# The last pair's evictions, additions and output sums in halves, two evictions shared by ACT and VectorE

## The reference

```
x = x + conv(x, w0) + ctx0(cond) + bias            # grouped conv, 4 groups, 9 taps
x = x + agg_w1(cond) @ x + agg_b1(cond)            # 128x128 matrix per sequence, a softmax blend of 8 experts
x = x + conv(x, w2) + ctx2(cond) + bias
x = x + agg_w3(cond) @ x + agg_b3(cond)
```

## Time and profile before

| | |
|---|---|
| median of 3 runs | 2497.8 us (2497.75 to 2498.95) |
| the profiled execution's own time | 2493.67 us |
| its span | 2491.9 us |
| TensorE busy | 2460.8 us, 99% |
| VectorE busy | 2136.1 us, 86% |
| ACT busy | 1523.4 us, 61% |
| DMA, mean over the span | 143 GB/s |

### The profile page before, as it was taken

The page is one execution under the profiler, slowest core; times in us unless marked ns, Lnnn a source line. Parts: engine busy times, 40 slices in busy tenths (PEclk is TensorE's granted clock), DMA queues, the critical chain, the costliest instruction groups (busy, mean ns, idle before and its releaser), DMA issues.

```text
span 2491.9 us, 99092 instructions
## 1 busy us (share of the span) xinstructions
PE 2460.8 (99%) x45256; PEld 1402.0 (56%) x45256; DVE 2136.1 (86%) x796; ACT 1523.4 (61%) x1116; POOL 32.0 (1%) x28
## 2 busy tenths in 40 slices
PE   7999999999999999999999999999999999999998
PEld 3444444444555555555666666666666666666664
DVE  6988988889889889889889888898898898898883
ACT  5566666666666666666666666666666666666665
POOL 5000000000000000000000000000000000000000
PEclk9999999999999999999999999999999999999999
DMA  9444444444444444444444454444444444444433
GB/s 361 149 145 150 126 132 159 130 126 157 138 126 145 149 126 137 152 132 126 150 145 126 137 157 128 127 159 135 126 150 144 126 142 150 129 128 154 139 95 120
DMA packets 186682, 357.23 MB, mean 143 GB/s; under 512 B 12754, under 2 KB 143834, under 8 KB 154010
## 3 DMA queue, kind: packets, MB, share of 16 engines
q1 hardware_dynamic: 184824, 352.50, 45.2%
q10 hardware_dynamic: 1826, 4.23, 0.5%
HBM read 205.69 MB, written 150.99 MB: 143 GB/s over the span
## 4 chain that ended last, share of the span: by engine, by line
PE 97%; DMA 1%; ACT 1%; DVE 1%; issue 0%; SPq 0%; ACTq 0%
PE psum L373 61%; PE psum L441 35%; DMA mix_dram<-y 1%; DMA out<-outb 0%; ACT y L576 0%; DVE h L730 0%; PE psum L300 0%; ACT outb L625 0%; DVE y L727 0%; PE psum L347 0%; DVE diff L695 0%; DVE shared L738 0%; DVE y L738 0%; DVE y L750 0%; ACT y L612 0%
## 5 line engine op out<-in xcount | busy, mean ns | idle before, releaser
L373 PE MATMUL psum<-diff,prod_w 32*64 32x512 f32 x28672 | 1684.0, 588 | 8.0 <-ACT y L576 2.5
L373 PEld LDWEIGHTS psum<-diff,prod_w 32*64 32x64 f32 x28672 | 908.1, 131 | 684.4 <-issue 401.9
L695 DVE TENSOR_TENSOR diff<-xin 128x2052 f32<-128x2052 f32 x256 | 994.0, 3929 | 288.4 <-PE psum L373 288.4
L441 PE MATMUL psum<-y,mixw 32*64 32x512 f32 x16384 | 1020.1, 588 | 5.5 <-ACT y L576 3.4
L441 PEld LDWEIGHTS psum<-y,mixw 32*64 32x64 f32 x16384 | 545.8, 131 | 371.2 <-issue 221.1
L695 DVE TENSOR_TENSOR diff<-x 128x2055 f32<-128x2055 f32 x256 | 571.2, 2299 | 4.7 <-ACT x L664 4.7
L625 ACT ACTIVATE outb<-psum,bias_now 128x2048 f32<-128x2048 f32 x129 | 252.2, 1956 | 197.9 <-PE psum L441 196.3
L664 ACT ACTIVATE x<-psum,bias_now 128x2048 f32<-128x2048 f32 x128 | 252.8, 1975 | 195.4 <-PE psum L441 195.4
L603 ACT COPY shared<-psum 128x2048 f32<-128x2048 f32 x128 | 239.1, 1868 | 170.4 <-PE psum L373 169.5
L748 DVE TENSOR_TENSOR y<-y,shared 128x2048 f32<-128x2048 f32 x128 | 293.1, 2290 | 38.2 <-ACT y L614 38.2
L616 ACT COPY y<-psum 128x2048 f32<-128x2048 f32 x128 | 239.2, 1869 | 93.6 <-PE psum L373 93.6
(11 more groups left out here) (61 smaller groups left out, 83.3 us busy)
## 6 DMA issues: line engine op xcount, KB each, us to landing
out<-outb SPq DMA_DIRECT2D x127, 1024.0 KB, 4.8
xin<-x SPq DMA_DIRECT2D x126, 1024.0 KB, 6.8
mixw<-mix_dram SPq DMA_DIRECT2D x508, 128.0 KB, 5.5
mix_dram<-shared SPq DMA_DIRECT2D x8, 1024.0 KB, 12.5
mix_dram<-y SPq DMA_DIRECT2D x8, 1024.0 KB, 12.0
xin<-x ACTq DMA_DIRECT2D x2, 1024.0 KB, 10.9
y<-experts ACTq DMA_DIRECT2D x2, 512.0 KB, 4.6
prod_w<-conv_w SPq DMA_DIRECT2D x4, 256.0 KB, 7.9
```

The source lines that it names most:

```text
L373: return pe.matmul(psum[cols, half, g, :], prod_w[v][at, kind, s, cols], moving, start=start, stop=stop, skip_group_check=True)
L441: mm = pe.matmul(psum[cols, half, r, :], mixw[home][at, b, g, cols], y[home][at, :, g, b, :], start=g == 0, stop=g == GROUPS - 1)
L695: nc.vector.tensor_tensor(into(kind), in0, in1, op).then_inc(diff_ready[v], 1)
```

## The change

All of it is in the steps from the first mixing of the last pair (63) on. TensorE's order of matmuls, the number of matmuls and all that is computed stay as they are.

- **x2 of sequence 1**: ACT evicts phases 0 and 1 (signal `x2_ready`), VectorE phases 2 and 3 by `tensor_scalar` (signal `x2_upper`, in `last_diffs`). TensorE waits for both before conv, ACT for `x2_upper` too before it overwrites `bias_now`.
- **BOTH** is added in two halves of columns (phases 0 and 1, then 2 and 3), with a signal each; conv waits for the second half behind its fourth set (`second`). The counts for SIGNED and ONLY_ODD go up by one.
- **half_mix(1, 1)** waits only for line 612's copy at first, for 614's before the TRAILING rows.
- **take_sums** copies the second result half in two pieces, the first at `conv_done` 7.
- **outputs** makes four half operations (groups 0 and 1, groups 2 and 3) with a signal each; `half_mix(0, 0)` waits for the third at first, for the fourth before the TRAILING rows.
- **The last eviction**: ACT evicts phases 0 and 1, VectorE phases 2 and 3 (`last_out`, signal `out_upper`), both over all m. Each of the two stores waits for both. SP stores the upper half of the positions, ACT issues the store of the lower half.

```diff
@@ -138,6 +138,8 @@
...
         x2_ready = sem("x2_ready")
+        x2_upper = sem("x2_upper")
+        out_upper = sem("out_upper")
         out_ready = sem("out_ready")
@@ -195,6 +197,15 @@
...
             return {BOTH: diff2[:, 0], SIGNED: diff2[:, 1], ONLY_EVEN: diff0[:, 0], ONLY_ODD: diff0[:, 1]}[kind]
+
+        def x2_of(b, phases):
+            into = x2[:].rearrange("p (j c) -> p j c", j=PAR)[:, :, 0:PH * T]
+            into = into.rearrange("p j (r b m) -> p j r b m", r=PH, b=PB)[:, :, phases, b, 0:R]
+            return into, psum[:, b, :, :].rearrange("p r (j m) -> p j r m", j=PAR)[:, :, phases]
+
+        def out_of(b, phases):
+            return (outb[:, b, :].rearrange("p (m j r) -> p m j r", j=PAR, r=PH)[:, :, :, phases],
+                    psum[:, b, :, :].rearrange("p r (j m) -> p m j r", j=PAR)[:, :, :, phases])
@@ -243,10 +254,9 @@
...
                         if whole(i) and i == PAIRS + 1 and b == PB - 1:
-                            for part in range(2):
-                                sp.wait_ge(out_ready, PB * PAIRS + part)
-                                at = slice(part * L // 2, (part + 1) * L // 2)
-                                sp.dma_start(out[B - 1, :, at], outb[:, b, at]).then_inc(out_stored[b], 16)
+                            sp.wait_ge(out_ready, PB * PAIRS)
+                            sp.wait_ge(out_upper, 1)
+                            sp.dma_start(out[B - 1, :, L // 2:L], outb[:, b, L // 2:L]).then_inc(out_stored[b], 16)
                             continue
@@ -367,6 +377,9 @@
...
+            def nothing():
+                pass
+
             def conv_tile(v, kind, half, s, g, cols, start=False, stop=False):
@@ -386,7 +399,7 @@
...
-            def conv(v, n, a_free, b_free, diffs, late, halves=(A, B_HALF)):
+            def conv(v, n, a_free, b_free, diffs, late, halves=(A, B_HALF), second=nothing):
@@ -397,6 +410,7 @@
...
                 wide_set(v, BOTH, A, 0, TRAILING, start=True)
+                second()
                 wide_set(v, BOTH, A, 2, LEADING)
@@ -462,11 +476,14 @@
...
-            def half_mix(b, home, late):
+            def half_mix(b, home, late, second=nothing):
...
                 late()
-                for g in range(1, GROUPS):
+                mix_set(1, b, b, 1, LEADING, home)
+                second()
+                mix_set(1, b, b, 0, TRAILING, home)
+                for g in range(2, GROUPS):
                     mix_set(1, b, b, g, LEADING, home)
@@ -475,9 +492,6 @@
...
                 mix_set(m, B_HALF, 1, GROUPS - 1, TRAILING).then_inc(mix_done[m], 1)
-
-            def nothing():
-                pass
@@ -498,14 +512,15 @@
...
                 half_mix(0, 1, lambda: mix_tail(0))
+                pe.wait_ge(x2_upper, 1)
                 conv(1, n, (x2_ready, PB * PAIRS), (out_ready, PB * (n - 1) + 1),
-                     (PRODUCTS * n + 1, PRODUCTS * n + 2, PRODUCTS * n + 4), lambda: half_mix_tail(0, 1),
-                     halves=(B_HALF, A))
-                pe.wait_ge(sums_taken[1], COPIES * n + 2)
-                half_mix(1, 1, lambda: conv_tail(1, A))
-                pe.wait_ge(y_ready[1], 2 * PAIRS)
+                     (PRODUCTS * n + 1, PRODUCTS * n + 3, PRODUCTS * n + 5), lambda: half_mix_tail(0, 1),
+                     halves=(B_HALF, A), second=lambda: pe.wait_ge(diff_ready[1], PRODUCTS * n + 2))
+                pe.wait_ge(sums_taken[1], COPIES * n + 1)
+                half_mix(1, 1, lambda: conv_tail(1, A), lambda: pe.wait_ge(sums_taken[1], COPIES * n + 2))
+                pe.wait_ge(y_ready[1], 2 * n + 3)
                 pe.wait_ge(mix_loaded[0], MIX_LOADS * (PAIRS + 1))
-                half_mix(0, 0, lambda: half_mix_tail(1, 1))
+                half_mix(0, 0, lambda: half_mix_tail(1, 1), lambda: pe.wait_ge(y_ready[1], 2 * n + 4))
                 pe.wait_ge(out_ready, PB * n)
@@ -612,25 +627,28 @@
...
                 nc.scalar.copy(into[:, 0, 2:4], psum[:, A, 2:4, :]).then_inc(sums_taken[v], 1)
+                if whole(n) and v == 1 and n == PAIRS - 1:
+                    act.wait_ge(conv_done[v], done + 7)
+                    nc.scalar.copy(into[:, 1, 0:2], psum[:, B_HALF, 0:2, :]).then_inc(sums_taken[v], 1)
+                    act.wait_ge(conv_done[v], done + 8)
+                    nc.scalar.copy(into[:, 1, 2:4], psum[:, B_HALF, 2:4, :]).then_inc(sums_taken[v], 1)
+                    return
                 act.wait_ge(conv_done[v], done + 8)
...
-            def give_out(i, b, parts=1):
+            def give_out(i, b, phases=slice(0, PH)):
                 n = i - 2
...
                     act.wait_ge(out_stored[b], 16 * n)
-                for part in range(parts):
-                    at = slice(part * R // parts, (part + 1) * R // parts)
-                    nc.scalar.activation(
-                        outb[:, b, :].rearrange("p (m j r) -> p m j r", j=PAR, r=PH)[:, at],
-                        psum[:, b, :, :].rearrange("p r (j m) -> p m j r", j=PAR)[:, at], ACT.Identity,
-                        bias=bias_now[:, b, 1:2]).then_inc(out_ready, 1)
+                nc.scalar.activation(*out_of(b, phases), ACT.Identity, bias=bias_now[:, b, 1:2]).then_inc(out_ready, 1)
...
                         act.wait_ge(x2_ready, PB * i)
+                        if whole(i) and i == PAIRS:
+                            act.wait_ge(x2_upper, 1)
                     else:
@@ -647,7 +665,10 @@
...
                     else:
-                        give_out(i, 1, parts=2)
+                        give_out(i, 1, phases=slice(0, PH // 2))
+                        act.wait_ge(out_ready, PB * PAIRS)
+                        act.wait_ge(out_upper, 1)
+                        act.dma_start(out[B - 1, :, 0:L // 2], outb[:, 1, 0:L // 2]).then_inc(out_stored[1], 16)
                     return
@@ -659,10 +680,9 @@
...
                         act.wait_ge(mix_done[0], PB * i + b + 1)
-                        into = x2[:].rearrange("p (j c) -> p j c", j=PAR)[:, :, 0:PH * T]
-                        into = into.rearrange("p j (r b m) -> p j r b m", r=PH, b=PB)[:, :, :, b, 0:R]
-                        nc.scalar.activation(into, psum[:, b, :, :].rearrange("p r (j m) -> p j r m", j=PAR),
-                                             ACT.Identity, bias=bias_now[:, 2 * PB + b, 0:1]).then_inc(x2_ready, 1)
+                        phases = slice(0, PH // 2 if whole(i) and i == PAIRS - 1 and b == 1 else PH)
+                        nc.scalar.activation(*x2_of(b, phases), ACT.Identity, bias=bias_now[:, 2 * PB + b, 0:1]
+                                             ).then_inc(x2_ready, 1)
@@ -744,13 +764,52 @@
...
                 dve.wait_ge(shared_ready[v], COPIES * n + 3)
+                if whole(n) and v == 1 and n == PAIRS - 1:
+                    mid = GROUPS // 2 * BANK
+                    dve.wait_ge(sums_taken[v], COPIES * n + 1)
+                    nc.vector.tensor_tensor(flat[:, 0, 0:mid], flat[:, 0, 0:mid], kept[:, 1, 0:mid], ALU.subtract
+                                            ).then_inc(y_ready[v], 1)
+                    dve.wait_ge(sums_taken[v], COPIES * n + 2)
+                    nc.vector.tensor_tensor(flat[:, 0, mid:], flat[:, 0, mid:], kept[:, 1, mid:], ALU.subtract
+                                            ).then_inc(y_ready[v], 1)
+                    dve.wait_ge(sums_taken[v], COPIES * n + 3)
+                    nc.vector.tensor_tensor(flat[:, 1, 0:mid], flat[:, 1, 0:mid], kept[:, 0, 0:mid], ALU.add
+                                            ).then_inc(y_ready[v], 1)
+                    dve.wait_ge(sums_taken[v], COPIES * n + 4)
+                    nc.vector.tensor_tensor(flat[:, 1, mid:], flat[:, 1, mid:], kept[:, 0, mid:], ALU.add
+                                            ).then_inc(y_ready[v], 1)
+                    return
                 dve.wait_ge(sums_taken[v], COPIES * n + 2)
...
+            def last_diffs():
+                n = PAIRS - 1
+                dve.wait_ge(mix_done[0], PB * PAIRS)
+                dve.wait_ge(picked, PAIRS)
+                nc.vector.tensor_scalar(*x2_of(1, slice(PH // 2, PH)), bias_now[:, 2 * PB + 1, 0:1], None, ALU.add
+                                        ).then_inc(x2_upper, 1)
+                dve.wait_ge(x2_ready, PB * PAIRS)
+                size, mid = PH * T - 1, PH // 2 * T
+                for at in (slice(0, mid), slice(mid, size)):
+                    if at.start:
+                        dve.wait_ge(x2_upper, 1)
+                    nc.vector.tensor_tensor(diff_of(1, BOTH)[:, at], x2[:, at], x2[:, HALF + at.start:HALF + at.stop],
+                                            ALU.add).then_inc(diff_ready[1], 1)
+                diff_of_x2(n, (SIGNED, ONLY_EVEN, ONLY_ODD))
+
+            def last_out():
+                dve.wait_ge(mix_done[1], PB * PAIRS)
+                dve.wait_ge(picked, PAIRS + 2)
+                dve.wait_ge(out_stored[1], 16 * (PAIRS - 1))
```

(9 more changed lines are left out.)

## The result

The changed kernel's median is 2489.24 us (11 runs, 2487.87 to 2491.36). The ratio is 0.9977, with a 95% interval of 0.9969 to 0.9985: 0.23% or 5.7 us faster, between 3.7 and 7.7. I had forecast a gain of 5.3 us, which holds, and a time of 2492.5 in a range from 2491.3 to 2495.0, which doesn't: the measured time lies 2.1 us under it.

The account below looks back on a forecast made before the run. TensorE, busy nearly throughout, was taken as the bound, so only its waits could give time back. Terms 3.05 + 0.28 + 1.77, one restart fewer and 0.1 at the end made 5.3: 2497.8 - 5.3 = 2492.5 us, range 2491.3 to 2495.0.

Parts of the forecast that it names:

- I carry the difference over: Whole kernel: the 4.1 us between the runs' median 2497.8 and the profiled 2493.67 stays, so 2497.8 - 5.3 = 2492.5.
- Part 1 and 2: Before the last pair's conv: halved x2 eviction and BOTH remove the 1.89 us stall; the clock stays up, saving 2.1 us.
- The clock term: Conv's first ten sets in the last pair: at full clock 4.3 us instead of 6.4, 2.1 us saved, bounds 0 and 2.1.
- Part 3: Last pair's conv: TensorE newly stalls 0.9 us for ONLY_ODD; the third difference wait is passed 3.05 us earlier.
- Part 4: Last two half_mix: divided sums and copies remove stalls of 0.28 and 1.77 us; one restart fewer saves 0.1 to 0.2.
- Part 5: Kernel's end: bytes decide, so dividing the last eviction gains 0 to 0.1 us; VectorE's piece costs 1.22, at most 2.0 to 2.2.
- The clock rival: Last pair: clock falls after the new stall or elsewhere, or earlier runs mostly lacked the fall; gain 3.2 us, chance 0.2.
- The doubled last eviction: Kernel's end: VectorE's last eviction takes double, both stores wait, bytes stand still 0.9 us; gain 4.4 us, chance 0.17.
- a change without effect: Last pair: slow VectorE eviction or engines holding each other up leave differences late; gain about 2 us, chance 0.05.
- The store on ACT's queue: Kernel's end: this store lands late, making the kernel 1.7 to 4.1 us slower; decides from 9.2 us landing, chance 0.03.

## Why the prediction was right or wrong

**What failed.** The step "The median of the runs is 2497.8, 4.1 above it. I carry the difference over". The three runs shown lay at the top of the spread; 33 later runs of the kernel before have a median of 2494.17 (2490.92 to 2497.73). The eight other runs measured beside the changed kernel have 2494.55. The difference that I added, 4.1 us, is 0.5 to 0.9 against these medians: the three runs were a high draw, and nothing on record says why. The profiled execution's own 2493.67 was the better base: 2493.67 - 5.3 = 2488.4, 0.9 from the measured median. And the range took in the unknown prices of the change but not the start of the kernel, which moves t0 by up to 5.2 us between executions. I read the row of 60 to 2440 us, a mean of 1.00, and so had both the 0.91 of 60 to 80 us and TensorE's wait before the first mixing averaged away. The chances (0.48 faster, 0.5 the same, by 5.0 us) were near: the gain of 5.7 lies just beyond, its interval on both sides.

**Part 1 and 2: right, with two sizes off.** VectorE's tensor_scalar on 1024 columns of PSUM takes 1.28 us where I took 1.22; ACT's half took 1.12 beside it, against 1.11 alone, so it was not held up; VectorE's piece alone is in no run. The stall went from 1.89 to 0.16 and the clock stayed up. The rest of the stall, which I had put at nothing, is 0.16. The clock term was mis-sized, 2.1 for 1.70; it is shown to be the stall's doing by the run with matmuls in its place.

**Part 3: right.** ONLY_ODD became the next thing late, at t0 + 10.19 (2464.26), as I had it (2463.83 with t0 at 2453.64). The delay is 0.69, not 0.95. The three terms 1.9 + 2.1 - 0.95 = 3.05 measured 1.73 + 1.70 - 0.69 = 2.74.

**Part 4: right, undersized.** 2.59 for 2.05 + 0.1: the restarts, whose "0.1 to 0.2" no row or run shows; it is about 0.25 each.

Together: 2.73 + 2.59 = 5.32 at outb[0]'s eviction (28.84 - 23.53 = 5.31), where I had 5.2. That the sum fits so closely is luck: 0.3 too much in the first three parts and 0.4 too little in the fourth cancel.

**Part 5: right in that the bytes decide** in this kernel, so the division of the last eviction is worth nothing: 0.0 against the 0 to 0.1 that I gave it. Its price that I couldn't read is now seen: VectorE's last piece, with a jump at every element in PSUM, takes 1.28 us, exactly as long as the one for x2 with runs of 256. ACT's took 1.17 instead of 1.11. The Trainium skill ("SBUF — State Buffer", the note on cachelines in "Door 1: The DMA port swizzle") gives PSUM lines of two fp32 values and says of non-contiguous access there that it slows down matmuls. That VectorE's read would pay too was my extension of it, and this trace shows no such penalty: 1.28 us either way.

**The rivals.** The clock rival failed in its first form; no stretch fell in any of the seven profiles with x2 divided. In its second form (the runs of before mostly lack the fall) it failed as well: it was there in all three profiles of before. The doubled last eviction and a change without effect failed. The store on ACT's queue landed 4.3 us after its issue, where the one on SP's took 3.8, far from the 9.2 at which it would have decided.

## What to carry to other kernels

Before a gain of a few parts in a thousand is set against a time, look where the executions of the kernel themselves differ: here TensorE's busy time in the loop was constant to 1 us, while the first 80 us moved the whole by 5, through the landing of one store and through the clock. Compare such edits from a milestone behind the noisy stretch to the end. Price a stall of TensorE at its length, a quarter microsecond for the restart and, where the windows show one, the half clock stretch behind it (1.70 us for the stall of 1.89, nothing for the one of 1.77). At the end of a kernel look at the bytes by windows: while they flow without a gap, only an earlier first byte shortens the end and a quicker last eviction gives nothing; once they run out before the last stores, these and the last eviction set the end.

## What the runs showed of the hardware

- A stall of 1.89 us was followed by about 3.4 us at half clock in each of the four profiles that had it, one of 1.77 or 1.78 us in none of the five that had that one. With matmuls in place of the first, the stretch was gone. The two stalls stand in different places, so that their length decides is not shown.
- VectorE's tensor_scalar from PSUM, 1024 f32 columns per partition, takes 1.28 us whether it reads runs of 256 or jumps at every element, both times beside an ACT eviction from other banks.
- Two 512 KB stores issued together on SP's and ACT's queues behind a 1 MB store finished at the same time as two on SP's queue alone, 1 us apart (6.12 and 6.10 us from the start of the last eviction). From 2483.5 to 2485.5 us 403 GB/s flowed, about as the 401 before; the window of 379 above takes in the end of the stream.
